# A two-layer transformer block on one core: the stages of the first pass stand in another order on the five engines

## The chip, the cores and the metric

The kernel runs on one core of a Trainium2 chip. The metric is the time of one execution in microseconds (us), as the median of three runs. Lower is better.

The core has engines that each work through a queue of instructions of their own, strictly in the order in which the program put them there: TensorE (PE: matrix products and transposes), VectorE (DVE), ScalarE (ACT: exponentials, other functions and copies), GpSimd (POOL), and SyncE (SP), which here only issues transfers. An engine that comes to a wait stands until a semaphore has the value asked for, and all behind it stands too.

## The reference

Two layers over 2 x 1024 tokens of 256 features. In each layer attention and a feed-forward part both read the normalised input, and both are added to it:

```python
xn = _layernorm(x)
x = x + _L0_attn_ref(xn, Wq, bq, ..., bo) + _L0_ffn_ref(xn, w_gating, w_linear)
xn = _layernorm(x)
x = x + _L1_attn_ref(xn, wq, wk, wv, wo, inv_freq) + _L1_ffn_ref(xn, w_gate_up, w_proj)
...
# _L0_attn_ref: 32 query heads and 8 key/value heads of 8 features, rotary, causal over all 1024 tokens
scores = jnp.einsum('bhqd,bhkd->bhqk', q, k_rep) / scale
scores = jnp.where((kpos > qpos)[None, None], -jnp.inf, scores)
attn = jax.nn.softmax(scores, axis=-1)
# _L0_ffn_ref: fp8 operands
activations = jax.nn.gelu(_qdot(x, w_gating[0])) * _qdot(x, w_gating[1])
outputs = _qdot(activations, w_linear)
# _L1_attn_ref: for each token, 16 heads attend to the 16 heads of the same token
scores = jnp.einsum('bshd,bstd->bsht', q, k) / jnp.sqrt(jnp.float32(HD))
# _L1_ffn_ref: weights quantised to three values per group of 64, silu gate, rms norm
h = jax.nn.silu(gate) * up
return jnp.einsum('bsh,dh->bsd', rms_norm(h), wq_p)
```

## The kernel before

The 2048 tokens are 16 tiles of 128. The work on a tile is cut into stages, each a small function of the kernel, and a step is a stage with a number, as `qk.119` or `wo1.8`. Where a stage comes once per tile the number is the tile's.

Layer 0, attention: `ln0`, `rs0` and `xn` normalise; `xnT` transposes on PE, `xnTc` copies the result out of PSUM (L1178, L1180); `qkv` projects (L625, L626), `qkvc` adds the bias; `rope` (POOL) rotates; `qh`, `ql`, `q0` and `kl` split into parts for 16-bit products; `qxT` turns them and `kTc`, `qTc` copy them out. The scores are computed in 144 quads, two for each pair of a query tile and a key tile at or before it: `qk.Q` (PE, L685, four products of 512 columns, one into each of the four banks of psS), `exp.Q` (ACT, L958, two instructions over two banks each), `mask.Q` on the diagonal (POOL, L1645), and `pv.Q` (PE, L699, eight records in the trace). `qk.Q+1` may write its first two banks only when the first half of `exp.Q` has read them, and its last two when the second half has. So ACT is never more than one quad behind PE, and never ahead. `ob`, `obT`, `att`, `attT`, `wo0` and `xa` finish the attention of a tile.

Layer 0, feed-forward: `up` (L736) four times a tile, `g`, `sq`, `ge1`, `th`, `fh`, `ge3` for the gelu, `down` (L750), `yff`, `xf`. The weights come as six pieces: SP's `wg.k` loads one into half of the tile `stage` (L495, L498), DVE's `w8.k` makes it fp8 (L1104). `up` waits for four of them.

Layer 1: `ln1`, `rs1`, `xn1`, `xn1T`, `xn1Tc`; `qkv1` (L775); `qk1c`, `v1c`, `ro1`, `ro1p`, `ro2`; a way through DRAM (`vw`, `vr`); `gT` (L788), `S1` (L821), `ex1` (L1016), `PV1` (L832), `o1r`, `o1T`, `o1`, again through DRAM (`ow`, `at1r`), `at1T`, `wo1` (L853, L854). Its feed-forward: `gu` (L866), `tg`, `sg`, `hh`, `ssq`, `ssm`, `rsg`, `hxa`, `hx`, `hxT` (L876), `hTc`, `dn1` (L885), and then `yo`, `yout`, `out`. Once: `tc`, `ts`, `tsc`, `td`, `tde`, `tr`, `tw` quantise the weights of that part; `wh` (ACT, L995) and `wl` split the weights of `qkv1`, which a transfer has brought (L484; its semaphore also counts the transfer of wo1, L485); `tab` and `sin` (L924) make the table of angles; `vz` (L1067) clears the tile of values.

What stands where in each engine's queue is written out by hand in the dictionary `ORDER`: one string of steps for each engine, 791 on PE, 421 on ACT, 692 on DVE, 146 on POOL and 88 on SP. Each engine walks its string:

```python
ahead = e.mark_branch_hint_location()
for name, n in first_pass("pe"):
    run[name](n)
```

Each step makes its own waits. Most PE stages fill one of three PSUM banks (psA, psB, psC) in turn, in the order of the string, and wait until the fill three places before has been read:

```python
if k >= len(psM):
    before, number = fills[k - len(psM)]
    w.wait_ge(*EMPTIED[before](number))
```

A second pass with other stages runs only if a flag asks for it; in these runs it doesn't.

Matmuls are of three shapes: over the whole array (most stages), in four groups of 32 rows (`qk`, `S1`), and in four groups of 32 columns (`pv`, `PV1`). The prediction calls a change from one shape to another a shape change.

Of the kernel before, what the change touches and what calls it, by code (L numbers as in the profile page):

```python
# [49 lines left out]
        "xnT.0 qkv.0 ts.0 xnT.1 xnT.2 qkv.1 ts.1 qxT.0 qxT.1 qk.0 xnT.3 qk.1 qkv.2 up.0 up.1 up.2 qxT.2 pv.0 qxT.3 "  # L50
        "up.3 qk.2 pv.1 qk.3 pv.2 qk.4 pv.3 qk.5 obT.0 pv.4 qkv.3 qxT.4 qxT.5 qk.6 pv.5 td.0 xnT.4 qk.7 pv.6 up.4 "
        "td.1 up.5 qk.8 tr.0 pv.7 attT.0 qk.9 pv.8 obT.1 qk.10 pv.9 up.6 up.7 qk.11 down.0 tr.1 xnT.5 attT.1 qkv.4 "
        "qxT.6 ts.2 up.8 qxT.7 up.9 pv.10 pv.11 qk.12 ts.3 up.10 qkv.5 qk.13 pv.12 wo0.0 qk.14 pv.13 down.1 qk.15 "
        "qxT.8 xnT.6 up.11 pv.14 qk.16 pv.15 wo0.1 qk.17 pv.16 up.12 td.2 pv.17 qk.18 td.3 qkv.6 qk.19 tr.2 qxT.9 "
        "up.13 down.2 tr.3 up.14 obT.2 pv.18 pv.19 qk.20 ts.4 ts.5 xn1T.0 obT.3 qk.21 pv.20 up.15 qk.22 qxT.10 pv.21 "
        "up.16 up.17 qk.23 td.4 td.5 up.18 up.19 tr.4 tr.5 attT.2 pv.22 qk.24 xn1T.1 qxT.11 pv.23 ts.6 ts.7 qkv1.0 "
        "wo0.2 qk.25 pv.24 td.6 td.7 up.20 tr.6 qk.26 tr.7 attT.3 down.3 pv.25 qk.27 ts.8 ts.9 gu.0 pv.26 qk.28 "
        "pv.27 up.21 td.8 td.9 qk.29 xnT.7 tr.8 tr.9 pv.28 qk.30 qxT.12 wsum.0 wsum.1 qkv1.1 ts.10 ts.11 pv.29 qk.31 "
        "up.22 pv.30 qk.32 up.23 obT.4 pv.31 qk.33 pv.32 td.10 td.11 wo0.3 tr.10 tr.11 gu.1 gu.2 attT.4 qk.34 pv.33 "
        "gu.3 qk.35 gu.4 qkv.7 qk.36 pv.34 pv.35 gT.0 down.4 gT.1 gu.5 qk.37 gu.6 pv.36 qk.38 qkv1.2 hxT.0 xnT.8 "  # L60
        "S1.0 pv.37 qxT.13 xn1T.2 hxT.1 qk.39 gu.7 qkv1.3 xnT.9 up.24 qk.40 pv.38 pv.39 PV1.0 qk.41 qxT.14 gu.8 "
        "qkv.8 o1T.0 pv.40 qk.42 up.25 xnT.10 qkv1.4 wo0.4 gu.9 xn1T.3 qk.43 pv.41 gT.2 gu.10 up.26 pv.42 qk.44 gT.3 "
        "qkv1.5 at1T.0 qkv1.6 up.27 qk.45 pv.43 pv.44 qxT.15 up.28 gu.11 qk.46 gu.12 up.29 wo1.0 S1.1 pv.45 pv.46 "
        "qk.47 up.30 dn1.0 qk.48 pv.47 hxT.2 down.5 qk.49 gT.4 up.31 xn1T.4 pv.48 qk.50 gT.5 hxT.3 pv.49 qk.51 pv.50 "
        "PV1.1 S1.2 qxT.16 qkv.9 o1T.1 qk.52 pv.51 qkv1.7 up.32 qk.53 up.33 obT.5 pv.52 qk.54 PV1.2 pv.53 qk.55 "
        "attT.5 o1T.2 down.6 gu.13 at1T.1 qk.56 pv.54 pv.55 wo1.1 obT.6 gu.14 gu.15 qk.57 pv.56 up.34 qxT.17 qk.58 "
        "xnT.11 dn1.1 gT.6 up.35 qk.59 pv.57 pv.58 up.36 hxT.4 hxT.5 qk.60 up.37 qkv.10 qkv1.8 gT.7 down.7 qk.61 "
        "pv.59 pv.60 xnT.12 up.38 up.39 qk.62 at1T.2 qkv1.9 wo0.5 gu.16 S1.3 qxT.18 wo1.2 pv.61 qk.63 pv.62 gu.17 "
        "qk.64 pv.63 up.40 up.41 qk.65 pv.64 qxT.19 up.42 qk.66 pv.65 gu.18 gT.8 qk.67 dn1.2 qk.68 pv.66 pv.67 gT.9 "
        "up.43 hxT.6 qk.69 pv.68 PV1.3 qk.70 attT.6 up.44 down.8 hxT.7 S1.4 pv.69 pv.70 qk.71 xn1T.5 wo0.6 o1T.3 "  # L70
        "up.45 qk.72 qkv1.10 gu.19 qk.73 pv.71 qkv.11 down.9 qk.74 pv.72 PV1.4 pv.73 qk.75 at1T.3 xnT.13 up.46 gu.20 "
        "up.47 qk.76 pv.74 pv.75 qxT.20 wo1.3 obT.7 qxT.21 o1T.4 qk.77 dn1.3 attT.7 gu.21 pv.76 qk.78 gu.22 up.48 "
        "pv.77 qk.79 up.49 obT.8 gu.23 hxT.8 qkv.12 xn1T.6 pv.78 qk.80 at1T.4 qkv1.11 up.50 gu.24 attT.8 qk.81 pv.79 "
        "pv.80 wo0.7 hxT.9 obT.9 qk.82 up.51 down.10 qkv1.12 pv.81 qk.83 qxT.22 qxT.23 qkv.13 qk.84 pv.82 down.11 "
        "up.52 xn1T.7 pv.83 qk.85 wo1.4 pv.84 qk.86 attT.9 wo0.8 xnT.14 qxT.24 pv.85 pv.86 qk.87 dn1.4 up.53 qk.88 "
        "gu.25 gu.26 obT.10 pv.87 qk.89 qkv1.13 qkv1.14 qxT.25 up.54 qk.90 pv.88 up.55 hxT.10 gu.27 pv.89 qk.91 "
        "hxT.11 gu.28 gT.10 qk.92 pv.90 wo0.9 attT.10 pv.91 qk.93 gT.11 gT.12 qkv1.15 xn1T.8 qkv.14 up.56 xnT.15 "
        "S1.5 pv.92 pv.93 qk.94 qxT.26 qxT.27 gT.13 gu.29 gu.30 obT.11 qk.95 pv.94 PV1.5 qk.96 up.57 qkv1.16 S1.6 "
        "attT.11 gu.31 up.58 wo0.10 qk.97 pv.95 xn1T.9 up.59 qkv1.17 o1T.5 qk.98 pv.96 pv.97 gT.14 gT.15 qk.99 pv.98 "
        "PV1.6 gu.32 S1.7 o1T.6 down.12 at1T.5 qk.100 pv.99 qxT.28 wo1.5 hxT.12 dn1.5 hxT.13 qk.101 qxT.29 gT.16 "  # L80
        "qkv1.18 at1T.6 qk.102 pv.100 PV1.7 pv.101 qk.103 qkv1.19 up.60 o1T.7 gT.17 wo1.6 dn1.6 S1.8 pv.102 pv.103 "
        "qk.104 gu.33 hxT.14 hxT.15 qk.105 pv.104 down.13 qk.106 obT.12 up.61 pv.105 qk.107 gu.34 gu.35 qk.108 "
        "pv.106 pv.107 gu.36 at1T.7 qk.109 pv.108 qkv.15 qk.110 pv.109 wo1.7 attT.12 qk.111 pv.110 xn1T.10 up.62 "
        "up.63 qk.112 pv.111 PV1.8 qk.113 hxT.16 wo0.11 dn1.7 qk.114 pv.112 pv.113 gT.18 gu.37 gT.19 o1T.8 gu.38 "
        "qk.115 gu.39 pv.114 qk.116 pv.115 qkv1.20 qk.117 hxT.17 wo0.12 gu.40 S1.9 pv.116 pv.117 qk.118 qkv1.21 "
# [1697 lines left out]
```

## Time and profile before

| what | us |
|---|---|
| three runs | 598.49, 600.28, 602.88 |
| median | 600.28 |
| span of the profiled execution | 601.7 |
| PE busy | 562.0 |
| ACT busy | 469.6 |
| DVE busy | 426.6 |
| POOL busy | 233.6 |

The profiled execution is a single one. Its record gives its span, from the first instruction to the last, and no other time for it; the span is 1.4 us above the median and inside the range of the three runs, so what lies around it is too small to be told from the scatter. Busy times overlap between engines. Ends of matmuls are modelled: the record of a matmul lasts longer than the distance to the next start, so a stall shorter than about that overhang hides inside busy time. For PE the distances from start to start tell more than the busy share.

### The profile page before, as it was taken

The page shows a single profiled execution, that of the slowest core. Times are in us where ns is not written, and L with a number is a line of the kernel's source. Part 1 is how long each engine was busy: PE and PEld are TensorE (multiplying, and loading weights), DVE is VectorE, ACT ScalarE, POOL GpSimd, SP SyncE. Part 2 cuts the span into 40 slices and gives each one's busy share as a digit, 9 for nine tenths or more (in the row PEclk, how much of TensorE's full clock was granted, in tenths as well). Part 3 has the DMA queues.
Part 4 walks back from the last instruction along what each step waited for, and adds up shares of the span by engine and source line. Part 5 has one row for each costly group of instructions (what it writes and reads, how often), then busy time and mean ns, then how long its engine had stood idle before and what let it go on. Part 6 is the DMA issues. An engine that isn't in the chain of part 4 may idle for free. (4 is left out here: it accounts for less than half of the span.)

```text
span 601.7 us, 13300 instructions
## 1 busy us (share of the span) xinstructions
PE 562.0 (93%) x5153; PEld 290.7 (48%) x5153; DVE 426.6 (71%) x909; ACT 469.6 (78%) x607; POOL 233.6 (39%) x302
## 2 busy tenths in 40 slices
PE   3687898999999999999999999999999999999976
PEld 1332434433555555645544555565445454456654
DVE  5658889988789558856699877565555365658765
ACT  2378899999988997999878898777979877972631
POOL 3748666043533163306855641360232150250100
PEclk9778999999999999999999999999999999999989
DMA  8810101102041223030110330531301304035632
GB/s 265 303 36 2 36 1 35 36 2 49 6 62 33 33 59 39 27 37 3 19 17 2 64 54 27 89 55 27 54 10 36 45 20 69 17 68 85 94 57 48
DMA packets 150914, 30.40 MB, mean 51 GB/s; under 512 B 133952, under 2 KB 149568, under 8 KB 150848
## 3 DMA queue, kind: packets, MB, share of 16 engines
q1 hardware_dynamic: 150272, 29.19, 24.4%
q8 instruction: 42, 0.69, 0.5%
q10 hardware_dynamic: 576, 0.33, 0.3%
q14 instruction: 24, 0.20, 0.1%
HBM read 19.02 MB, written 10.49 MB: 49 GB/s over the span
## 5 line engine op out<-in xcount | busy, mean ns | idle before, releaser
L958 ACT ACTIVATE Pt<-psS 128x1024 f32<-128x1024 f32 x288 | 281.7, 1047 | 44.8 <-PE psS L685 25.9
L699 PE MATMUL psV<-Pt,vaug 128*32 128x512 f32 x1152 | 150.3, 611 | 0.3 <-POOL Pt L1645 0.3
L1645 POOL TENSOR_SCALAR_AFFINE_SELECT Pt<-Pt 128x1024 f32<-128x1024 f32 x64 | 71.7, 1145 | 43.8 <-ACT Pt L958 43.8
L685 PE MATMUL psS<-qTf,kTf 32*128 32x512 f16 x576 | 74.9, 390 | 7.3 <-ACT Pt L958 3.7
L685 PEld LDWEIGHTS psS<-qTf,kTf 32*128 32x128 f16 x576 | 20.3, 91 | 82.9 <-ACT Pt L958 48.1
L1695 POOL TENSOR_TENSOR ss<-ss,mhalf 128x1 f32<-128x1 f32 x16 | 9.5, 596 | 111.3 <-DVE ss L1476 111.3
L699 PEld LDWEIGHTS psV<-Pt,vaug 128*32 128x32 f32 x1152 | 25.7, 109 | 41.9 <-issue 35.9
L1016 ACT ACTIVATE stage<-psS 128x1024 f32<-128x1024 f32 x32 | 31.0, 1020 | 8.1 <-PE psS L821 7.9
L1686 POOL TENSOR_TENSOR r<-qk,cos 128x256 f32<-128x256 f32 x16 | 11.9, 744 | 63.9 <-ACT qk L991 58.0
L866 PE MATMUL psB<-wguT,xhs 128*128 128x512 bf16 x108 | 27.8, 380 | 0.0
L1032 ACT ACTIVATE qtmp<-qtmp 128x1024 bf16<-128x1024 f32 x16 | 16.9, 1059 | 12.9 <-PE psA L876 8.4
L1318 DVE SCALAR_TENSOR_TENSOR gw<-gw,gb 128x512 f32<-128x512 f32 x32 | 24.9, 781 | 2.5 <-ACT gw L973 2.5
L1327 DVE SCALAR_TENSOR_TENSOR ga<-gw,gb 128x512 bf16<-128x512 f32 x32 | 23.6, 738 | 3.9 <-ACT gw L984 3.8
L1636 POOL TENSOR_TENSOR QXf<-rt,QXf 128x512 f16<-128x512 f32 x16 | 19.1, 1195 | 18.1 <-ACT QXf L945 18.1
L1608 POOL TENSOR_SCALAR rs<-mv 128x1 f32<-128x1 f32 x16 | 5.3, 329 | 49.6 <-DVE mv L1164 49.6
L1625 POOL TENSOR_TENSOR rt<-qkv,cs 128x320 f32<-128x320 f32 x16 | 14.7, 916 | 24.5 <-DVE QXf L1220 15.8
L984 ACT ACTIVATE gw<-gw 128x512 f32<-128x512 f32 x32 | 21.2, 661 | 3.0 <-DVE gw L1318 2.9
L1482 DVE SCALAR_TENSOR_TENSOR qtmp<-qtmp,ss 128x1024 f16<-128x1024 f32 x16 | 21.4, 1336 | 2.9 <-ACT qtmp L1037 2.9
L866 PE MATMUL psC<-wguT,xhs 128*128 128x512 bf16 x88 | 22.8, 382 | 0.0
L973 ACT ACTIVATE gw<-gb 128x512 f32<-128x512 bf16 x32 | 21.2, 670 | 0.1
L885 PE MATMUL psA<-wpT,stmp 128*128 128x256 bf16 x176 | 21.1, 273 | 0.0
L1628 POOL TENSOR_TENSOR rt<-qkv,sn 128x160 f32<-128x160 f32 x32 | 20.9, 673 | 0.0
(381 smaller groups left out, 1246.5 us busy)
## 6 DMA issues: line engine op xcount, KB each, us to landing
qkvscr<-rqkv SPq DMA_DIRECT2D x16, 384.0 KB, 2.5
G<-qkvscr SPq DMA_DIRECT2D x24, 128.0 KB, 3.7
stage<-in_wg SPq DMA_DIRECT2D x4, 512.0 KB, 8.8
w8g<-qkvscr SPq DMA_DIRECT2D x16, 128.0 KB, 3.8
oscr<-o SPq DMA_DIRECT2D x16, 128.0 KB, 3.3
at<-oscr SPq DMA_DIRECT2D x16, 128.0 KB, 2.0
out<-yout SPq DMA_DIRECT2D x16, 128.0 KB, 2.5
x<-in_x SPq DMA_DIRECT2D x1, 1536.0 KB, 12.2
```

Of the source, the lines that this page charges most:

```text
L685: e.matmul(psS[j], kd[32 * j:32 * j + k, h, 128 * at:128 * at + 128], qd[32 * j:32 * j + k, 4 * h:4 * h + 4, :].rearrange("p s n -> p (s n ...
L699: ins = e.matmul(psV[32 * j:32 * j + 32, :], vaug[:, at, j, 32 * h:32 * h + 32], Pt[(4 * Q + j) % NP], start=(kb == 0 and h == 0), stop=(k ...
L866: ins = e.matmul(bank[:], src[:, pt, 128 * c:128 * c + 128], wguT[:, c, c0:c0 + 512], start=(k == 0), stop=(k == 3))
L885: ins = e.matmul(bank[:, 0:256], hT[:, pt, s, :], wpT[:, s, :], start=(k == 0), stop=(k == 15))
L958: e.activation(flat(Pt4[:, u % NP:u % NP + 2, :]), flat(psS4[:, j:j + 2, :]), ACT.Exp, scale=scale).then_inc(S["exp"], 1)
L973: e.activation(gw[:, half, :], gb[:, half, :], ACT.Square).then_inc(S["sq"], 1)
L984: e.activation(gw[:, half, :], gw[:, half, :], ACT.Tanh, scale=GC * GA).then_inc(S["th"], 1)
L1016: e.activation(P1[:, 4 * b:4 * b + 8, :].rearrange("p g n -> p (g n)"), flat(psS4[:, b:b + 2, :]), ACT.Exp, scale=SC1).then_inc(S["ex1"], 1)
L1318: e.scalar_tensor_tensor(gw[:, half, :], gw[:, half, :], 1.0 / GA, gb[:, half, :], ALU.add, ALU.mult).then_inc(S["ge1"], 1)
L1327: e.scalar_tensor_tensor(a, gw[:, half, :], 1.0, gg, ALU.add, ALU.mult).then_inc(S["ge3"], 1)
L1482: e.scalar_tensor_tensor(hx_b[:, 1, :], h1, sn[:, 2:3], hx_b[:, 0, :], ALU.mult, ALU.subtract).then_inc(S["hx"], 1)
L1645: e.affine_select(out=p, in_=p, pattern=[[0, 8], [1, 128]], compare_op=ALU.is_ge, fill=0.0, base=0, channel_multiplier=-1).then_inc(S["mas ...
```

## The change

Only the strings of `ORDER` differ. Each holds the same steps, and steps of one stage keep their own sequence; 34 to 87 steps of each string stand at the same place as before, the others have moved, on PE by 3.9 places on average and by 32 at most. The bank that a PE stage fills follows from its place, so many stages use another of the three banks than before. The file is four lines shorter, so that line L958 of before is L954 in the changed kernel, and so on for all lines behind the strings.

```diff
 ORDER = {
     "pe": (
-        "xnT.0 qkv.0 ts.0 xnT.1 xnT.2 qkv.1 ts.1 qxT.0 qxT.1 qk.0 xnT.3 qk.1 qkv.2 up.0 up.1 up.2 qxT.2 pv.0 qxT.3 "
...
+        "xnT.0 qkv.0 xnT.1 qkv.1 xnT.2 qxT.0 qxT.1 qk.0 ts.0 ts.1 up.0 qk.1 qxT.2 qkv.2 qxT.3 pv.0 qk.2 up.1 xnT.3 "
...
     "sp": (
-        "wt.2 wg.2 wg.3 wg.4 wg.5 wt.3 wt.4 wt.5 vw.0 vr.0 vw.1 vr.1 ow.0 at1r.0 vw.2 vr.2 vw.3 ow.1 at1r.1 out.0 "
...
+        "wg.2 wg.3 wg.4 wg.5 wt.2 wt.3 wt.4 wt.5 vw.0 vr.0 vw.1 ow.0 at1r.0 vr.1 vw.2 vr.2 ow.1 at1r.1 vw.3 vr.3 out.0 "
...
```

ACT at the start, before: the two instructions of `tc.0`, then `qh.0`, the four of `exp.0` and `exp.1`, `qh.1`, `g.0`, `fh.0`.

```order
L931 ACTIVATE qtmp<-r 128x1024
L932 ACTIVATE qtmp<-r 128x1024
L945 ACTIVATE QXf<-rt 128x32x16
L958 ACTIVATE Pt<-psS 128x1024 x4
L945 ACTIVATE QXf<-rt 128x32x16
L966 ACTIVATE gb<-psC 128x512
```

The same place now; the row over 1536 columns is `wh.0`.

```order
L927 ACTIVATE qtmp<-r 128x1024
L928 ACTIVATE qtmp<-r 128x1024
L941 ACTIVATE QXf<-rt 128x32x16
L991 ACTIVATE wqkv<-stmp 128x1536
L954 ACTIVATE Pt<-psS 128x1024 x2
L941 ACTIVATE QXf<-rt 128x32x16
L962 ACTIVATE gb<-psA 128x512
```

`wh.0` has moved from the 61st place of ACT's string to the third, ahead of `exp.0`. `sin.0`, which was the 17th step, is the 102nd.

DVE between the bias of the first tile and the copies of the second, before (`qkvc.0`, `xnTc.1`, `xn.3`, `tsc.0`, `w8.0`, `xnTc.2`, `w8.1`):

```order
L1189 TENSOR_TENSOR qkv<-psB,bqkv 128x384
L1178 COPY xnT<-psA 128x256
L1180 CAST x8T<-psA 128x256
L1171 TENSOR_SCALAR xn<-x,mv_1,rs_1 128x256
L1130 TENSOR_SCALAR qtmp<-psC 128x512
L1104 CAST w8g<-stage 128x1024
L1178 COPY xnT<-psB 128x256
L1180 CAST x8T<-psB 128x256
L1104 CAST w8g<-stage 128x1024
```

And now:

```order
L1185 TENSOR_TENSOR qkv<-psB,bqkv 128x384
L1100 CAST w8g<-stage 128x1024 x2
L1174 COPY xnT<-psC 128x256
L1176 CAST x8T<-psC 128x256
L1167 TENSOR_SCALAR xn<-x,mv_0,rs_0 128x256
```

Both casts `w8.0` and `w8.1` now stand ahead of `xnTc.1`; `vz.0`, which stood between `ln0.0` and `xn.0`, is now the first step of DVE.

PE in the last quarter, from `qk.119` to `qk.120`, before: `PV1.9` and `pv.118` stand between them.

```order
L685 MATMUL psS<-qTf,kTf 128x512 x4
L832 MATMUL psC<-stage,w8l 32x128 x16
L699 MATMUL psV<-Pt,vaug 32x512 x4
L685 MATMUL psS<-qTf,kTf 128x512 x4
L699 MATMUL psV<-Pt,vaug 32x512 x4
```

And now, with `wo1.8`, `xn1T.11` and `pv.118` between them:

```order
L681 MATMUL psS<-qTf,kTf 128x512 x4
L849 MATMUL psC<-wo,at1T 128x256
L850 MATMUL psC<-wo,at1T 128x256
L586 MATMUL psA<-identf,xn_1 128x128
L587 MATMUL psA<-identf,xn_1 128x128
L695 MATMUL psV<-Pt,vaug 32x512 x4
L681 MATMUL psS<-qTf,kTf 128x512 x4
```

`PV1.9`, of the same shape as `pv.118`, has gone from beside it, and two stages over the whole array have come.

## Rows read from the trace of the kernel before

**Rows 1.** The page: span, and busy time of each engine.

```profile
span 601.7 us, 13300 instructions
PE 562.0 (93%) x5153; PEld 290.7 (48%) x5153; DVE 426.6 (71%) x909; ACT 469.6 (78%) x607; POOL 233.6 (39%) x302
```

**Rows 2.** Busy time by stretch: stretch, length, PE, PEld, DVE, ACT, POOL, clock, DMA, GB/s.

```profile
0.00:22.20 22.20, 8.93 (x27) 4.31 (x28) 14.05 (x35) 3.92 (x4) 10.24 (x25) 1.00 0.94 304
22.20:48.10 25.90, 21.02 (x130) 8.70 (x130) 14.44 (x36) 18.43 (x24) 15.09 (x16) 0.74 0.25 90
48.10:111.35 63.25, 56.85 (x464) 24.80 (x465) 56.93 (x108) 59.01 (x82) 40.74 (x51) 0.97 0.06 18
111.35:225.95 114.60, 113.06 (x1032) 54.97 (x1029) 86.44 (x187) 105.56 (x139) 43.17 (x56) 1.00 0.21 37
225.95:532.70 306.75, 303.05 (x2851) 156.60 (x2850) 204.59 (x433) 255.22 (x325) 113.01 (x142) 1.00 0.23 37
532.70:602.00 69.30, 59.07 (x659) 41.29 (x657) 50.19 (x113) 27.44 (x37) 11.32 (x16) 0.98 0.39 66
```

**Rows 3.** Timeline of PE: start, length, instruction, count of records.

```profile
405.66 0.61 PE L736 MATMUL psC<-x8T,w8g 128*128 128x128 fp8e4 x8
406.11 0.61 PE L841 MATMUL psA<-identf,o1r 128*128 128x128 f32 x4
...
407.93 1.91 PE L885 MATMUL psA<-wpT,stmp 128*128 128x256 bf16 x16
409.77 1.17 PE L821 MATMUL psS<-qk1T 24*128 24x128 f32 x32
...
591.50 1.91 PE L885 MATMUL psA<-wpT,stmp 128*128 128x256 bf16 x16
593.25 0.27 PE L590 MATMUL psB<-identf,at 128*128 128x128 f32 x1
```

**Rows 4.** Timeline from qk.119 to qk.120, with idle time before and its releaser.

```profile
460.18 0.53 PE L685 MATMUL psS<-qTf,kTf 32*128 32x512 f16 x4
460.64 1.94 ACT L958 ACTIVATE Pt<-psS 128x1024 f32<-128x1024 f32 x2 [0.37 <-PE psS L685]
...
461.54 1.04 PE L699 MATMUL psV<-Pt,vaug 128*32 128x512 f32 x8
462.51 0.21 PEld L685 LDWEIGHTS psS<-qTf,kTf 32*128 32x128 f16 x4 [0.84 <-ACT Pt L958]
```

**Rows 5.** Timeline of the start, all engines.

```profile
1.25 0.41 SPq L470 DMA_DIRECT2D wqkv<-in_wqkv  x1
...
4.87 2.19 DVE L1067 MEMSET vaug<- 128x2560 f32 x1 [0.48 <-issue]
...
7.86 0.45 SPq L495 DMA_DIRECT2D stage<-in_wg  x1
...
10.63 1.62 PE L625 MATMUL psB<-wqkv,xnT 128*128 128x384 f32 x2 [2.23 <-DVE xnT L1178]
...
14.63 0.59 SPq L485 DMA_DIRECT2D wo<-in_wo  x1
...
22.64 3.77 ACT L958 ACTIVATE Pt<-psS 128x1024 f32<-128x1024 f32 x4 [4.17 <-PE psS L685]
...
25.98 0.69 DVE L1104 CAST w8g<-stage 128x1024 fp8e4<-128x1024 f32 x1 [3.93 <-DMA stage<-in_wg]
...
35.55 1.02 ACT L958 ACTIVATE Pt<-psS 128x1024 f32<-128x1024 f32 x1 [0.16 <-PE psS L685]
```

**Rows 6.** Transfers issued at 1.25, 7.86 and 14.63 us: size, us to landing.

```profile
wqkv<-in_wqkv SPq DMA_DIRECT2D x1, 384.0 KB, 6.5
...
stage<-in_wg SPq DMA_DIRECT2D x1, 512.0 KB, 7.5
...
wo<-in_wo SPq DMA_DIRECT2D x1, 256.0 KB, 8.8
```

**Rows 7.** ACT by line: busy, mean ns, idle before.

```profile
L995 ACT ACTIVATE wqkv<-stmp 128x1536 f16<-128x1536 f32 x1 | 1.7, 1677 | 0.0
L924 ACT ACT_TABLE_LOAD x1 | 1.3, 1283 | 0.0
```

255 rows, old and new, of the table ORDER are left out of this document.

## The prediction, made before the run

> **What bounds the kernel now.** I read the page first. PE is busy 562.0 of 601.7 us, ACT 469.6, DVE 426.6 [rows 1]. Then the busy time by stretch, cut where `qk.0`, `qk.6`, `qk.24`, `qk.56` and the end of the quads stand: the reader is to see that PE is busy 113.06 of 114.60 us and 303.05 of 306.75 us in the two middle stretches, but 8.93 of 22.20, 21.02 of 25.90 and 59.07 of 69.30 at the ends [rows 2]. PE bounds the middle, and the waits of start and end are chains through several engines.
>
> Busy isn't packed, though. In the timeline `qk.120` starts 2.33 us after `qk.119`, where its weight load has waited for ACT's exponentials of the quad before, and the busy share doesn't show it [rows 4]. A quad's two exponentials take 1.94 us [rows 4], and since the four score banks hold one quad only, `qk.Q+1` can't finish its writes sooner. So two things make PE's time in the middle: the work itself, and stalls at `qk` where ACT is late.
>
> **Prices on PE**, from start to start. Eight matmuls of 128 columns take 0.45 us, 405.66 to 406.11 [rows 3]. Sixteen of 256 columns take 1.75, 591.50 to 593.25, when a stage of the same shape follows, and 1.84, 407.93 to 409.77, when one of four row groups does [rows 3]: a shape change costs 0.09. `pv` with the change to `qk` behind it is 0.97, 461.54 to 462.51 [rows 4]; I take 0.87 and 0.1. Four row groups run together, so a `qk` is one stream of 512 columns; from the 128-column price that is 4 x 0.056, or 0.22 (an estimate). In this way each stage gets its number of columns times 0.44 ns. On ACT a quad is 1.94, `wh` 1.7 [rows 7], the other stages 0.6 to 1.2 by their width. All PE stages are priced at the full clock.
>
> With these I added up the written-out strings, once for each order. In each gap from one `qk` to the next, P is the PE work with its shape changes, A the ACT work from one `exp` to the next. Where A is over P, ACT falls behind; E is the sum of what it is over.
>
> - qk.6 to qk.24: P 50.2 before, 49.4 now; E 20.9, now 14.2. It took 63.25 [rows 2], so 13.0 were stalls.
> - qk.24 to qk.56: P 105.2, now 110.6; E 17.8, now 18.7. It took 114.60 [rows 2], stalls 9.4.
> - qk.56 to the last quad: P 283.8, now 282.9; E 31.8, now 19.4. It took 306.75 [rows 2], stalls 23.0.
>
> **The start, up to qk.6.** No row shows the new order, so I walk it with the prices of the old. `vz` (2.19 us [rows 5]) leaves the way of the first normalisation and runs while DVE would wait for its first data. The first projection could then start when its weights have landed, at 1.25 + 6.5 = 7.75, and not at 10.63 [rows 5, 6]: a gain of 2.9. The gain is held up twice. `w8.1` now stands ahead of `xnTc.1`, and its piece lands at 7.86 + 7.5 = 15.4 [rows 5, 6]; with the cast (0.69 [rows 5]) DVE goes on at about 16.1, so the second tile is no earlier than before and `qk.0` comes at about 22.5. And `wh.0` stands ahead of `exp.0`. It waits for both transfers of its semaphore, the last at 14.63 + 8.8 = 23.4 [rows 5, 6], and takes 1.7: `exp.0` starts at 25.1, where it was 22.64 [rows 5]. That costs 2.5.
>
> After that the new order is the looser one. Before, `exp.2` came only at 35.55 [rows 5], since DVE stood 3.93 us for the third piece of weights [rows 5], `up.0` to `up.2` stood ahead of `pv.0` on PE, and three of ACT's stages of the first `up`s stood behind that. Now one `up` stands there. In my walk kl.1 is done at 28.6, ql.1 on POOL at 29.5 (it has slipped behind both masks of `mask.0`), and `exp.2` starts near 32; `qk.6` comes near 45, with `wh` and one `th` out of the way, where it was at 48.1 [rows 2]. The walk is an estimate and can be 3 us off. Its bounds: a loss of the 2.5 if all behind `exp.0` keeps its distance, a gain of the 4.9 us in which PE is idle in this stretch, 25.90 less 21.02 [rows 2]. I take -3.
>
> The two table loads around `sin.0` (1.3 each [rows 7]) and its two instructions, 3.2 in all, stood ahead of `exp.6` and stand ahead of `exp.32` now, so they are in A of 24 to 56. They are neither saved nor added. Their cover there is ACT's idle time, 114.60 less 105.56 [rows 2]. Without it they would show fully.
>
> **The middle.** The bounds for each stretch: above, stalls go in proportion to E; below, only those go that the order forces, where P is under 2.3 us, the time from `qk` to `qk` that the exponentials need [rows 4]. There are 41 such gaps from qk.6 on, short by 6.1 us together, now 16, short by 2.6.
>
> - 6 to 24: in proportion 49.4 + 13.0 x 14.2 / 20.9 = 58.2, that is -5.0; the lower bound is -0.8 of work and -0.7 of short gaps, -1.5. I take -3.2.
> - 24 to 56: in proportion 110.6 + 9.9 = 120.5, +5.9; with the short gaps alone +5.4 - 0.9 = +4.5. I take +5.2.
> - 56 on: in proportion 282.9 + 14.0 = 296.9, -9.9; with the short gaps alone -0.9 - 1.9 = -2.8. I take -6.4.
>
> The middle of the bounds is a choice: some stalls have nothing to do with ACT, and E doesn't see them.
>
> P holds the shape changes. I counted them along PE's string: 431 before, 468 now, so 37 x 0.1 = 3.7 us more, which the sums above contain. A stage like PV1.9 has been taken from beside a `pv` of its own shape, as in the piece shown. The Trainium skill (TensorEngine Tiling (Array Packing), Tiling Modes) says it outright: "Changing tiling mode (not just tile) drains the TensorE". It names no price. By that rule alone, all else equal, the change would lose the 3.7.
>
> **The end.** The chain behind the last quad has the same work within 0.3 us (53.5 and 53.2 in my sum) in 69.3 us [rows 2]. `S1` and `ex1` of tiles 13 to 15 stand a little earlier, which helps the way through DRAM; `PV1.11` and `qkv1.28` are now behind the last quad, which doesn't. I take 0, with 2 us either way. The flag steps, now last, run while the last output is on its way.
>
> **Sum.** -3 (start) - 3.2 + 5.2 - 6.4 (middle) + 0 (end) = -7.4. The profiled span of 601.7 becomes 594.3. The median of the runs lies 1.4 under that span, so I say 593.
>
> **Rivals.**
>
> *Only PE's work counts* (chance 0.18). If ACT's lateness is absorbed, and stalls stay as they are, the middle changes by P alone, -0.8 + 5.4 - 0.9 = +3.7, and the start gives -3: about 601 on the median's scale, within 598 to 604. For it speaks PE's 99% in the middle [rows 2]; against it the waiting load at `qk.120` [rows 4].
>
> *Stalls follow E fully* (0.15). The upper bounds together: -3 - 5.0 + 5.9 - 9.9 = -12.0, with a start and an end 2 better each perhaps; 585 to 589.
>
> *`wh.0` holds up the whole start* (0.13), the case on the other side. All exponentials queue behind one transfer. If it lands at 23.4 or later and `exp.2` then keeps its distance to `exp.0` (which it does if mask.0 and ql.1 on POOL are the chain, from `exp.2` later than 35.55 on), the start loses 2.5 instead of gaining 3; with +3.7 of work that is not won back, 601.7 + 2.5 + 3.7 - 1.4 = 606.5.
>
> *The shape changes alone* (0.06). If neither start nor stalls move, 37 changes at the price of [rows 3] are left: 3.7 us more, 604, within 1%. This is what the Trainium skill's rule on tiling modes (same page and section) makes of the time when it is taken alone; the 0.09 that this trace shows agrees with the rule.
>
> **How the numbers follow.** My forecast is 589 to 598, with 593 as its centre and a chance of 0.48. A difference under 1% (6 us) can hardly be told from none with these runs. Under 594.3 lie the bigger gain, 0.15, and most of the lower half and centre of the forecast, 0.35: faster 0.50. Over 606.3 lies half of the wh case and little else; since the whole could drift in a way that no sum shows, I give slower 0.12, and the same 0.38. The range goes from 585, the full effect of E, to 604, where only work and drains count.
>
> **What the profile after would show.** `exp.0` at about 25, waiting through `wh.0` for a transfer; `qk.0` near 22.5; DVE standing about 3 us ahead of `w8.1`. `qk.6` near 45; qk.6 to qk.24 in about 60, qk.24 to qk.56 in about 120, the rest to `qk.143` in about 300. PE's waits for ACT ahead of `qk` are shorter in total. I am wrong if `exp.2` isn't ahead of 35.55, if the last long stretch takes 306 again, or if DVE or POOL, for which I added up nothing in the middle, now holds PE.

## The result, and the profile after

The changed kernel takes 631.41 us (median of 4 runs, 628.3 to 633.8) against 599.57 us: a ratio of 1.051, with an interval of 1.046 to 1.056. It is slower, and the forecast of 593 (585 to 604) was wrong by more than its range.

The page of the changed kernel, its first lines (beside [rows 1]), and the costliest groups of section 5. The changed kernel's line numbers are four lower than the old one's:

```profile
span 632.0 us, 13299 instructions
PE 562.5 (89%) x5153; PEld 288.8 (46%) x5153; DVE 452.0 (72%) x909; ACT 472.3 (75%) x607; POOL 241.9 (38%) x302
...
L954 ACT ACTIVATE Pt<-psS 128x1024 f32<-128x1024 f32 x288 | 279.5, 1026 | 57.1 <-PE psS L681 50.6
L695 PE MATMUL psV<-Pt,vaug 128*32 128x512 f32 x1152 | 154.7, 619 | 3.4 <-DVE ob L1286 3.3
L1641 POOL TENSOR_SCALAR_AFFINE_SELECT Pt<-Pt 128x1024 f32<-128x1024 f32 x64 | 76.2, 1215 | 92.0 <-ACT Pt L954 92.0
```

The same 909 instructions of DVE are busy 25.4 us longer. Nothing was added to them, so they last longer on the average: an engine was slowed, not loaded. POOL's masks last longer too; this is their line in the old kernel:

```profile
L1645 POOL TENSOR_SCALAR_AFFINE_SELECT Pt<-Pt 128x1024 f32<-128x1024 f32 x64 | 71.7, 1145 | 43.8 <-ACT Pt L958 43.8
```

Busy time by stretch, cut as in [rows 2] (start to `qk.0`, `qk.6`, `qk.24`, `qk.56`, `qk.143`, end), but each cut 0.25 us behind the quad's own start; columns as there:

```profile
0.00:21.58 21.58, 8.86 (x28) 4.52 (x28) 13.26 (x35) 3.92 (x4) 9.73 (x24) 0.84 0.91 310
21.58:50.35 28.77, 18.82 (x142) 8.22 (x138) 22.93 (x36) 19.03 (x25) 23.95 (x25) 0.78 0.23 83
50.35:113.41 63.06, 56.05 (x448) 24.32 (x444) 55.75 (x114) 54.32 (x74) 37.08 (x44) 0.94 0.06 18
113.41:245.10 131.69, 121.13 (x1066) 58.06 (x1064) 100.05 (x194) 112.48 (x146) 47.48 (x58) 0.96 0.20 34
245.10:560.48 315.38, 299.05 (x2828) 152.72 (x2824) 207.64 (x421) 256.31 (x325) 113.31 (x140) 0.98 0.21 35
560.48:632.00 71.52, 58.63 (x659) 40.94 (x655) 52.32 (x114) 26.26 (x35) 10.36 (x15) 0.97 0.38 64
```

From the quads' own starts (21.33, 50.10, 113.16, 244.85 and 560.23) the way to `qk.6` is 2.0 us longer than in the old kernel (-0.9 to `qk.0` and +2.9 behind it), the quads 6 to 24 take 0.2 less, the quads 24 to 56 17.1 more, 56 to 143 8.6 more, and the end 2.8 more. In the fourth stretch PE is idle for 10.6 us, where it was idle for 1.5. The granted clock is 0.96 and 0.98 in the fourth and fifth stretch, where it was 1.00.

One place shows how. The timeline of the changed kernel from 187.66 us, four engines (start, length, instruction; in brackets the idle time before it and who ended it):

```profile
188.13 2.32 POOL L1641 TENSOR_SCALAR_AFFINE_SELECT Pt<-Pt 128x1024 f32<-128x1024 f32 x2
...
188.26 1.24 DVE L1409 TENSOR_TENSOR rqkv<-r 128x256 f32<-128x256 f32 x1
...
189.42 1.30 DVE L1411 TENSOR_TENSOR rqkv<-r 128x256 f32<-128x256 f32 x1
...
190.83 0.43 DVE L1402 TENSOR_TENSOR r<-qk,sin 128x256 f32<-128x256 f32 x1
190.87 0.98 POOL L1682 TENSOR_TENSOR r<-qk,cos 128x256 f32<-128x256 f32 x1 [0.42 <-DVE rqkv L1411]
191.17 0.96 DVE L1403 TENSOR_TENSOR r<-qk,cos 128x256 f32<-128x256 f32 x1
...
192.05 0.55 DVE L1185 TENSOR_TENSOR qkv<-psC,bqkv 128x384 f32<-128x384 f32 x1
...
192.65 0.50 PEld L716 LDWEIGHTS psC<-wo,attT 128*128 128x128 f32 x2 [3.72 <-DVE qkv L1185]
192.65 1.22 PE L716 MATMUL psC<-wo,attT 128*128 128x256 f32 x2 [3.48 <-DVE qkv L1185]
193.66 1.06 PE L717 MATMUL psC<-wo,attT 128*128 128x256 f32 x2
194.52 1.06 PE L732 MATMUL psA<-x8T,w8g 128*128 128x128 fp8e4 x8
195.37 1.06 PE L732 MATMUL psB<-x8T,w8g 128*128 128x128 fp8e4 x8
196.36 1.92 PE L695 MATMUL psV<-Pt,vaug 128*32 128x512 f32 x8
198.22 0.40 PE L681 MATMUL psS<-qTf,kTf 32*128 32x512 f16 x4
```

In the old kernel the second of the two instructions of `ro2` stands at this length, and so does the first:

```profile
170.10 0.42 DVE L1415 TENSOR_TENSOR rqkv<-r 128x256 f32<-128x256 f32 x1
```

Read it from above. POOL's two masks run to 190.45, one behind the other, and the two instructions of `ro2`, 0.42 us in themselves, take 1.24 and 1.30. The second one of `ro1` takes 0.96 instead of 0.43: POOL's L1682 ends at 191.85, DVE's at 192.13, 0.28 later. `qkvc.8` stands behind all of them in DVE's row, bank psC isn't read until then, and `wo0.4` on PE waits 3.48 us for it. Of these the stretch of the three makes 2.2 (0.82 + 0.88 + 0.53 over their usual lengths); the rest is what else stands ahead of `qkvc.8`. Then PE works at the lower of its two clock levels for 5.6 us: eight fp8 products take 1.06 us, where they took 0.61 [rows 3], and a `pv` takes 1.92 instead of 1.04 [rows 4]. By the prices of the forecast this quad took about 6.5 us over its work, for one wait of 3.5.

**The 0.28 us come back everywhere.** I took for each line of DVE the length that its quickest fifth has, and listed each instruction over 0.12 us longer. There are 95 (53.1 us above their usual length), and 94 of them have an instruction of POOL beside them. 81 end a constant time after one of POOL's, to within 0.02 us, and the time is set by their own length: 0.28 us for the 43 of 0.42 or 0.43, 0.55 for the 20 of 0.68, 0.15 for the 7 of 0.28. Such a DVE instruction does its work only once POOL's has ended. The old kernel has 59 of them, with 27.9 us; under the masks alone it is 8.8 us before and 22.7 now.

Not every DVE instruction is held up so. In the changed kernel 235 of them start while one of POOL's has 0.2 us or more left. Of these, 111 read a PSUM bank and 20 are batch statistics, reductions and reciprocals in SBUF: none of the 131 is stretched. Of the other 104, which work from SBUF to SBUF, 86 are. `qkvc.8` in the rows above is of the first kind and keeps its usual 0.55 us beside POOL; it is late only by what stands ahead of it. So the steps that empty a bank aren't slowed themselves here: they are late behind others that are.

And it works in both directions. A mask takes 1.09 us at its usual length; 21 of the 64 take over 0.12 us more (7.5 us together; in the old kernel 7, with 3.2 us), and each of the 21 ends 0.95 us after the end of a DVE instruction. In this place the two engines hold each other up in turn:

```profile
139.68 2.58 POOL L1641 TENSOR_SCALAR_AFFINE_SELECT Pt<-Pt 128x1024 f32<-128x1024 f32 x2
...
139.90 1.41 DVE L1323 SCALAR_TENSOR_TENSOR ga<-gw,gb 128x512 bf16<-128x512 f32 x1
...
141.41 1.12 DVE L1326 TENSOR_TENSOR ga<-ga,fb 128x512 bf16<-128x512 bf16 x1
```

The first mask ends at 140.77, L1323 0.54 later at 141.31, the second mask 0.95 later at 142.26, and L1326 0.27 later at 142.53.

The Trainium skill (SBUF — State Buffer, Who interferes with whom) has this rule: the two engines share one pair of ports as an exclusive lock, held for the whole instruction, against a DVE instruction in a two-port mode or with two inputs in SBUF. Its "fully blocks (not throttle)" agrees with the constant 0.28 us.

The other waits are in the list of PE's waits over the changed kernel (us in total, times, the longest); in the old one no single wait behind the first normalisation and projection is longer than 1.8 us:

```profile
PE psC L716 <- DVE qkv L1185: 3.5, 1, 3.5
PE psV L695 <- DVE ob L1286: 3.3, 4, 1.6
PE psS L681 <- ACT Pt L954: 3.1, 4, 1.3
PE psA L784 <- DMA G<-qkvscr: 2.9, 1, 2.9
...
PE psB L784 <- DMA G<-qkvscr: 2.5, 1, 2.5
PE psC L586 <- DMA at<-oscr: 2.4, 1, 2.4
```

### The profile page after: what moved, and what is told of

It is laid out like the page before. It is cut to its first block, busy times and chain, and to the rows that moved or that the text cites. A ratio compares the mean times of both kernels' runs of the same rounds, so it can differ in the third digit from the quotient of the medians.

```text
span 632.0 us, 13299 instructions
## 1 busy us (share of the span) xinstructions
PE 562.5 (89%) x5153; PEld 288.8 (46%) x5153; DVE 452.0 (72%) x909; ACT 472.3 (75%) x607; POOL 241.9 (38%) x302
## 4 chain that ended last, share of the span: by engine, by line
PE 60%; DVE 19%; DMA 9%; issue 5%; SPq 3%; ACT 3%; DVEq 0%; ACTq 0%
PE psV L695 15%; PE psS L681 5%; DMA stage<-in_wg 3%; PE psC L862 2%; PE psB L862 2%; DMA G<-qkvscr 2%; DMA w8l<-qkvscr 2%; DVE ga L1326 2%; PE psA L862 2%; PE psS L817 2%; DVE ga L1323 2%; SPq L518 2%; DMA qkvscr<-rqkv 2%; PE psC L881 1%; PE psB L771 1%
## 5 line engine op out<-in xcount | busy, mean ns | idle before, releaser
L954 ACT ACTIVATE Pt<-psS 128x1024 f32<-128x1024 f32 x288 | 279.5, 1026 | 57.1 <-PE psS L681 50.6
L695 PE MATMUL psV<-Pt,vaug 128*32 128x512 f32 x1152 | 154.7, 619 | 3.4 <-DVE ob L1286 3.3
L1641 POOL TENSOR_SCALAR_AFFINE_SELECT Pt<-Pt 128x1024 f32<-128x1024 f32 x64 | 76.2, 1215 | 92.0 <-ACT Pt L954 92.0
L681 PE MATMUL psS<-qTf,kTf 32*128 32x512 f16 x576 | 61.2, 392 | 4.6 <-ACT Pt L954 3.1
L681 PEld LDWEIGHTS psS<-qTf,kTf 32*128 32x128 f16 x576 | 16.1, 91 | 75.8 <-ACT Pt L954 43.7
L1682 POOL TENSOR_TENSOR r<-qk,cos 128x256 f32<-128x256 f32 x16 | 12.6, 789 | 68.9 <-ACT qk L987 61.8
L1323 DVE SCALAR_TENSOR_TENSOR ga<-gw,gb 128x512 bf16<-128x512 f32 x32 | 26.1, 817 | 6.3 <-ACT gw L980 6.2
L1314 DVE SCALAR_TENSOR_TENSOR gw<-gw,gb 128x512 f32<-128x512 f32 x32 | 26.8, 838 | 1.8 <-ACT gw L969 1.8
L862 PE MATMUL psB<-wguT,xhs 128*128 128x512 bf16 x92 | 24.4, 389 | 0.0
L1326 DVE TENSOR_TENSOR ga<-ga,fb 128x512 bf16<-128x512 bf16 x32 | 21.8, 680 | 3.3
L1330 DVE CAST a<-ga 128x512 fp8e4<-128x512 bf16 x32 | 21.7, 679 | 1.1
## 6 DMA issues: line engine op xcount, KB each, us to landing
x<-in_x SPq DMA_DIRECT2D x1, 1536.0 KB, 12.1
```

The source lines that it names most:

```text
L681: e.matmul(psS[j], kd[32 * j:32 * j + k, h, 128 * at:128 * at + 128], qd[32 * j:32 * j + k, 4 * h:4 * h + 4, :].rearrange("p s n -> p (s n ...
L695: ins = e.matmul(psV[32 * j:32 * j + 32, :], vaug[:, at, j, 32 * h:32 * h + 32], Pt[(4 * Q + j) % NP], start=(kb == 0 and h == 0), stop=(k ...
L862: ins = e.matmul(bank[:], src[:, pt, 128 * c:128 * c + 128], wguT[:, c, c0:c0 + 512], start=(k == 0), stop=(k == 3))
L954: e.activation(flat(Pt4[:, u % NP:u % NP + 2, :]), flat(psS4[:, j:j + 2, :]), ACT.Exp, scale=scale).then_inc(S["exp"], 1)
L1314: e.scalar_tensor_tensor(gw[:, half, :], gw[:, half, :], 1.0 / GA, gb[:, half, :], ALU.add, ALU.mult).then_inc(S["ge1"], 1)
L1323: e.scalar_tensor_tensor(a, gw[:, half, :], 1.0, gg, ALU.add, ALU.mult).then_inc(S["ge3"], 1)
```

## The experiments

All kernels were compared with the old one on the same chip; it took 599.7 to 601.2 us beside them. The changed kernel ran only in the first comparison, so where an experiment is set against its 631.4 us, a difference of 2 us isn't clear of noise. The kernels of an experiment have the old kernel's line numbers, or up to a few more. "Small mask" kernels leave seven eighths of the causal mask out.

### Where the loss is made: four splices

```diff
# a24b, a60b: each engine's string = its changed order up to the last step that had started
#             when qk.24 (qk.60) began in the trace, then the rest in the old order
# b24a, b56a: the old order up to qk.24 (qk.56), then the rest in the changed order
```

> The changed order on every engine up to the steps that had started when quad 24's scores began (its first 24 quads of 144), the old order for all that is left. Theory P (the loss is made where the trace shows it: +2.1 us up to quad 24, +17.1 from 24 to 56, +8.6 from 56 to 143, +2.2 after): this kernel keeps only the first +2.1 us, so 602 us (600 to 604). Rival H (the start leaves behind something that the rest pays for, such as buffers and queues in another phase, DRAM transfers behind): 610 us or more.

> The old order up to quad 24's scores, the changed order for the rest. Theory P: the whole of the middle's and the end's loss, 600 + 17.1 + 8.6 + 2.2 = 628 us (625 to 631). Rival H: under 615 us.

> The changed order up to quad 60's scores, the old order for the rest. At quad 60 the changed kernel was 16.7 us behind. Theory P: 600 + 16.7 = 617 us (614 to 620). Rival H: 622 us or more, or the old order makes some of it good (under 612 us) where its waits had slack.

> The old order up to quad 56's scores, the changed order for the rest. Theory P: 600 + 8.6 + 2.2 = 611 us (608 to 614). Rival H (the tail stretch's own loss came from the 19 us of lateness that it took over): 600 to 604 us.

Measured: a24b 608.9 us (1.012 to 1.019 of the old kernel), b24a 629.7 (1.043 to 1.051), a60b 621.2 (1.032 to 1.037), b56a 622.7 (1.035 to 1.039). Compared with the old kernel at the same quads in the traces (the end is that of PE's last matmul), in us:

```
              quad 24   32     48     56     80     110    130    143    end
changed         1.8    8.6   18.1   18.9   19.2   19.8   29.5   27.5   31.1
b24a           -2.1    7.1   12.6   13.5   13.8   15.7   23.8   21.9   26.9
a60b            1.9    9.8   16.6   17.5   16.1   16.1   16.1   16.1   14.1
b56a           -0.6   -0.6   -0.6   10.5   10.3   10.9   18.4   16.4   18.6
a24b            6.2    7.1    6.9    6.9    6.7    6.7    6.7    6.7    4.6
```

The old order behind a seam holds its distance to a tenth of a us over 60 quads (a60b, 80 to 143), and the changed order makes its losses at the same places, whatever ran before. So theory P holds by the traces, with b24a inside its range in time. By the times alone it isn't as clear: a60b is 1 us above P's range and 1 under the rival's 622, and the other two expectations missed, a24b by 7 (it is nearer to the rival's 610) and b56a by 12 us. Both lose it in the quads just ahead of the seam (7.9 us from quad 12 to 24, and 11.1 from 48 to 56), where two orders that don't fit each other meet. A splice has a price of its own, and only the stretches away from its seam can be read.

### The masks, and the named waits

```diff
# after_small_mask, before_small_mask
-e.affine_select(out=p, in_=p, pattern=[[0, 8], [1, 128]], ...
+e.affine_select(out=p[:, 0:1, :], in_=p[:, 0:1, :], pattern=[[0, 1], [1, 128]], ...
# after_later_gathers: TensorE's string
-... hxT.12 gT.16 qxT.28 pv.100 qk.102 hxT.13 qxT.29 ...
+... hxT.12 qxT.28 pv.100 qk.102 hxT.13 qxT.29 gT.16 ...
# (gT.20 behind wo0.13, gT.22 behind pv.132 likewise; on VectorE gTq.10 two steps later)
# after_banks_first: VectorE's string, the first two of eight moves
-... ro2.1 ro1.2 qkvc.8 ...        -... ge3.21 sg.10 ...
+... qkvc.8 ro2.1 ro1.2 ...        +... sg.10 ge3.21 ...
```

> The changed kernel with the causal mask put on the first 128 of each 1024 columns only (the other seven eighths stay unmasked, so this part of the computation is left out): GpSimd's 128 mask instructions of the first pass shrink from about 1.2 us to some 0.3 us, everything else stays. Theory C (GpSimd's instructions, when they run beside VectorE's, stretch them: line 1326's 0.42 us to 0.9 us; in the changed order the masks fall on VectorE's long steps, and the emptying of TensorE's banks behind them comes late): the changed kernel gains far more from it than the old one does, 618 us or less here. Rival O (the order of the rows alone makes banks and transfers late, the stretch is a bystander): 626 to 632 us.

> The old kernel with the same cut (the mask on the first 128 of 1024 columns, the rest left out). Theory C: little to gain, 597 to 601 us, so that the distance to the changed kernel with the same cut falls from 31 us to 20 us or less. Rival O: the distance stays at 27 to 32 us.

> The changed kernel with three of its transposes of gathered tiles later in TensorE's row: gT.16 and gT.22 one to two quads later, gT.20 one quad later (and VectorE's gTq.10 two steps later with it). These three waited 2.5, 2.9 and 1.2 us for the gathering DMA, and the first two were followed by 3.6 and 5.8 us at the lower clock. Theory L (each loss is local, and the lower clock is its echo): 6.6 us of waits and some 4.7 us of the lower clock go, 620 us (618 to 624). Rival N (whoever is late next takes the time): 627 us or more.

> The changed kernel with eight steps of VectorE that empty TensorE's banks taken out from behind long steps and put ahead of them: qkvc.8 before ro2.1, wmin.0 before tw.6, sg.10 before ge3.21, hTc.8 before ge3.22, sg.11 before xn.14, yff.11 before ge3.25, xa.9 before ge3.26, hh.21 before xn1.12. TensorE's waits for them were 3.5, 1.7, 0.8, 1.0, 1.8, 1.2, 1.3 and 0.8 us, 12.1 us together, and 5.6 us at the lower clock followed the first. Theory L: 617 us (614 to 621). Rival N: 627 us or more.

Measured: 608.7 and 598.0 us for the small masks, 627.4 for the later gathers, 629.4 for the banks first. With small masks the changed order gains 22.7 us and the old one 3, and the distance falls from 31 to 10.7 us: theory C. The page of the changed order with small masks has DVE back at the busy time of the old kernel with whole masks, though not one of its instructions was touched:

```profile
span 609.6 us, 13299 instructions
PE 558.4 (92%) x5153; PEld 288.3 (47%) x5153; DVE 425.9 (70%) x909; ACT 471.7 (77%) x607; POOL 189.3 (31%) x302
```

The moves at the named waits gave 4 and 2 us where theory L had promised 11 and 14; with single runs from 625.1 to 631.6 the 2 us can't be told from nothing. In after_banks_first `wo0.4` waits no more, and behind it a product of `up` waits 2.75 us for the next DVE step of the same row. For 12.1 us of waits for DVE the time fell by 2. Rival N has it: a row that is late hands its lateness to the next step.

### Is it the stretch, or GpSimd's own row?

```diff
# after_small_mask_idle_work: behind each small mask
+for i in range(2):
+    w.wait_ge("dummy", len(dummies))
+    dummies.append(Q)
+    e.affine_select(out=idle[:, 0:448], in_=idle[:, 0:448], pattern=[[1, 448]], ...).then_inc(S["dummy"], 1)
# before_more_idle_work: the same behind each whole mask of the old kernel
# after_small_mask_one_long: instead of the two
+e.tensor_tensor(idle[:], idle[:], idle[:], ALU.add).then_inc(S["dummy"], 1)
# after_mask_halves, before_mask_halves (n = 4), after_mask_quarters (n = 2): whole masks in pieces
-e.affine_select(out=p, in_=p, pattern=[[0, 8], [1, 128]], ...
+for h in range(0, 8, n):
+    ins = e.affine_select(out=p[:, h:h + n, :], in_=p[:, h:h + n, :], pattern=[[0, n], [1, 128]], ...
```

> The changed kernel with the mask on the first 128 of 1024 columns only (the rest unmasked, so left out), and after each of these short masks GpSimd does two masks of 448 columns on a tile that nobody reads. TensorE gets its tile as early as with the small mask alone (608.7 us), but GpSimd is busy about as long as with the whole mask (631 us). Theory C (GpSimd's busy time beside VectorE is what costs): 622 us or more, and VectorE's line 1330 back from 0.43 us towards 0.68 us. Rival W (TensorE waited for the masks' results): 608 to 613 us.

> The old kernel with its masks whole, and behind each the same two masks of 448 columns on a tile that nobody reads: GpSimd works about 60 us more in the first pass. Theory C: the old order isn't proof against it but has more slack, since its masks stretched VectorE by only 8.6 us against 22.7 in the changed order; 604 to 615 us. Rival P (the old order puts nothing of VectorE near the masks by its nature): 600 to 603 us.

> The changed kernel, each whole mask of 1024 columns issued as two instructions of 512 (nothing left out). Theory E (a VectorE instruction that meets one of GpSimd's does its work only after that one has ended, so the length of one instruction counts): the masks' 22.7 us of stretch fall to about 12 and the time from 631 us to 618 to 625 us. Rival R (GpSimd's row is what is late): the row gets some 0.15 us longer per mask, 631 to 636 us.

> The old kernel with each mask issued as two instructions of 512 columns. Theory E: 598 to 601 us (with small masks it gained 3 us). Rival R: 601 to 605 us.

> The changed kernel with each mask issued as four instructions of 256 columns; GpSimd's mask time grows by about a third. Theory E: the stretch under masks falls to some 7 us; 612 to 622 us. Rival R: 634 us or more.

> As after_small_mask_idle_work (mask on 128 of 1024 columns, the rest left out), but the idle work behind each small mask is one addition of 512 bfloat16 columns (about 1.2 us) instead of two masks of 448 (0.6 us each); GpSimd is as busy. Theory E: VectorE's stretch goes from 31 us to 40 us or more and the time from 616.7 to 621 us or more. Rival R: 614 to 618 us, as with the two short ones.

Measured, with the stretch worked out as above (all of it, and what lies under the masks or under the idle work in their place) and the busy times of the page:

```
                              time    DVE busy  stretch  under them  POOL busy
changed kernel                631.4    452.0     53.1      22.7       241.9
after_mask_halves             624.6    441.7     43.3      15.6       254.6
after_mask_quarters           625.6    430.7     29.4       7.5       273.4
after_small_mask_one_long     621.4    440.4     41.5      17.4       261.4
after_small_mask_idle_work    616.7    430.9     31.3       8.7       265.3
after_small_mask              608.7    425.9     26.8     under 1     189.3
old kernel                    600      426.6     27.9       8.8       233.6
before_mask_halves            600.3    424.0     25.0       5.1       243.6
before_more_idle_work         649.0    437.2     37.8      19.5       311.0
before_small_mask             598.0    418.5     18.8     under 1     182.3
```

The halves were 7 us faster with 13 us more of POOL's time, as theory E has it and rival R excludes (1.034 to 1.044 of the old kernel, against 1.046 to 1.056). The quarters fulfil E's forecast for the stretch (7.5, forecast 7) and miss that for the time, 625.6 (one of four runs 631.6) instead of 612 to 622. Their list of PE's waits says what came in its place, POOL itself, which the changed kernel had at 0.2:

```profile
PE psV L699 <- POOL Pt L1646: 14.9, 14, 2.5
```

So both causes are real: the stretch of DVE, and a row of POOL that is itself late. With the idle work as one long instruction, an addition, the stretch is 10 us larger and the median 4.7 us later than with two short ones, although POOL is busy 4 us less; their single runs overlap (614.8 to 622.1 against 613.1 to 621.0), and they ran beside different measurements of the old kernel (601.1 and 599.7), so this pair only leans to E. After_small_mask_idle_work itself fell between its two forecasts, at 616.7. The idle work costs 8 us over small masks alone, with only 4.5 us more of stretch in all; the other 15 of the 22.7 went with the stretch and with the masks' earlier results, which these runs don't part.

Before_more_idle_work missed by far: I had expected 604 to 615. It took 649.0, and not by the stretch (10 us more), but because the idle work stands ahead of the next mask:

```profile
PE psV L700 <- POOL Pt L1648: 25.1, 15, 3.3
```

The old order isn't proof against a slow GpSimd. It is fitted to this one.

### The rest

```diff
# after_small_mask_gathers_sin: small mask, the three later gathers, and ScalarE's string
-... exp.20 ... exp.31 sin.0 g.11 exp.32 ...
+... exp.20 ... sin.0 exp.21 ... exp.31 g.11 exp.32 ...
# after_gathers_banks_sin: whole masks, with the eight moves of after_banks_first as well
# after_small_mask_gathers_old_tail: small mask, gathers, sin.0 not moved; from qk.143 on the old order
```

> The changed kernel with the small mask (seven eighths of it left out), the three later transposes of gathered tiles (gT.16, gT.20, gT.22, with gTq.10), and the step with the two sines ahead of quad 21's exponential instead of quad 32's. With the small mask alone 608.7 us; TensorE's waits for the gathers were 3.1, 2.8 and 1.5 us there with the lower clock behind two of them, and 1.3 us for the exponential behind the sines. If these are the rest of the distance to the old kernel with the small mask (598.0 us): 598 to 601 us. If others take their place: 605 us or more.

> The changed kernel, whole masks, with all the moves so far: the three later transposes, the eight bank emptyings ahead of long steps, and the sines earlier. Alone the first gave 4 us and the second 2 us. Theory C: while the masks stretch VectorE, moving its steps only passes the wait on, 621 to 626 us. Rival O (order alone): the moves act together once none is left to take over the wait, 612 us or less.

> The changed kernel with the small mask (seven eighths left out) and the three later transposes of gathered tiles, and from quad 143's scores on the old order on every engine. Theory T (the end's own order makes the loss there): the last stretch takes 64 to 65 us again instead of 71.0, the time 599 to 602 us. Rival D (the stretch before leaves a debt of transfers and GELU steps): the last stretch takes 68 us or more, 604 to 608 us.

Measured: 607.1, 625.4 and 600.3 us. The second is what moves of the order alone can do while the masks stretch DVE: 6 us of 31. The first gave only 1.6 us for the gathers and the sines, and its profile shows why. From quad 56 to 143 it took 303.5 us, where small masks alone gave 308.9 and the old kernel with small masks 305.5; but from `qk.143` to PE's last matmul it took 71.0 against 63.6. Its timeline has the end's own gathers there:

```profile
561.58 1.08 PE L788 MATMUL psC<-identf,G 128*128 128x128 f32 x4 [1.83 <-DMA G<-qkvscr]
574.72 0.33 PE L590 MATMUL psC<-identf,at 128*128 128x128 f32 x1 [2.49 <-DMA at<-oscr]
```

With the old order behind `qk.143` that stretch is 62.9 us and the time 600.3 (0.995 to 1.003 of the old kernel): theory T. With that the distance to before_small_mask (598.0) is down to 2.3 us. (Theory T had 64 to 65 us for the stretch.) No kernel here that computes the reference beats the old one; the best, before_mask_halves, is the same within its interval (0.997 to 1.002).

## Why the prediction was wrong

**The term that was missing.** The forecast said that it "added up nothing in the middle" for DVE and POOL, and named that as the way it would fail. That is the step that failed. I priced PE and ACT in each gap, and left DVE out because it had slack on the average (86.44 of 114.60 us [rows 2]). But the emptying of a bank isn't an average: it stands in one row, behind steps whose length depends on what POOL does at that moment. About 20 of the 31 us go with the masks: with small ones a distance of 10.7 is left. How much of the 20 is DVE's stretch and how much POOL's own lateness is open; the halves show that at least part of it, 7 us, is the stretch. The lower clock behind a long stall makes it dearer: between quads 24 and 143 the changed kernel works in four spells of 3.2, 5.6, 3.6 and 5.8 us at the lower level, behind PE's waits of 1.3 (the sines), 3.5, 2.5 and 2.9 us, and does half the work there. The old kernel has no such spell between these quads.

**The start, -3.** The first part of the walk was right: `qk.0` at 21.33 (forecast 22.5), `exp.0` near 24.2 (25.1) behind `wh.0`, which waited for its transfer, and `exp.2` ahead of its old 35.55, at 32.92 (32). Rows of ACT in the changed kernel, to be read against [rows 5]:

```profile
22.76 1.48 ACT L991 ACTIVATE wqkv<-stmp 128x1536 f16<-128x1536 f32 x1 [7.68 <-DMA wo<-in_wo]
24.15 1.92 ACT L954 ACTIVATE Pt<-psS 128x1024 f32<-128x1024 f32 x2
...
32.92 1.94 ACT L954 ACTIVATE Pt<-psS 128x1024 f32<-128x1024 f32 x2 [2.30 <-PE psS L681]
```

So the rival in which `wh.0` holds up the whole start is out: `exp.0` came 1.5 us later than before (priced at 2.5), and `exp.2` 2.6 earlier. But `qk.6` came at 50.1, not 45, behind a copy that took 1.08 us for 0.18 beside a mask and GELU steps of 1.37 and 1.20 for 0.68. With small masks it came at 45.6, near the forecast, but there the old kernel has 46.6; and four more profiled executions with small masks and the same order up to there have 45.2, 46.2 and, with idle work, 47.1 and 48.6. So of the -3 no gain is shown that is clear of this scatter, and with whole masks it is a loss of 2.0. A walk that prices each DVE step at its usual length finds the place and not the order's worth.

**Quads 6 to 24, -3.2.** Measured -0.2; with small masks 60.6 against 62.1, -1.5, the lower bound (60.6 is one execution; two others have 58.4 and 61.1).

**Quads 24 to 56, +5.2.** Measured +17.1, and +8.6 with small masks. If the work term of +5.4 is right, the rest of the 8.6 are stalls that the sum by ACT's excess doesn't see, as `wmin.0` (1.7 us at `ts.8`).

**The sines, neutral.** Not quite. ACT's two table loads (1.28 each) and sines stood between two exponentials, and PE waited 1.3 us for the second (its longest wait for ACT in the list above); the first of the four spells at the lower clock came behind it. Averaged idle time of ACT was named as their cover; it wasn't idle there. Moving them was never measured alone.

**Quads 56 on, -6.4.** Measured +8.6. With small masks alone it is +3.5. With the three gathers later as well it is -2.0 in one execution (303.5 us) and +0.4 in another (305.9, after_small_mask_gathers_old_tail, whose order is the same up to `qk.143`). So even the direction isn't shown. The ACT excess E fell by 12.4 us in the sum, and the stalls went from 21.7 to 20.6 or 23.0. That stalls follow E, on which the -6.4 rests, is not shown by any run, and the rival in which they follow it fully is out. What E could not see cost more: the gathers whose transfers were issued late, as `gT.16` and `gT.20`, 2.5 and 2.9 us of waiting.

**The shape changes, +3.7.** The price holds in the old trace: L885's sixteen products take 1.84 to 1.85 us in six places where four row groups follow, and 1.75 to 1.76 in eight where the whole array does. What 37 more of them cost the kernel no run isolates. PE's busy time in the two profiles is 562.5 and 562.0, with the lower clock in it, and doesn't settle it.

**The end, 0.** Measured +2.8 to the end of the span and +3.6 to PE's last matmul, and by the latter +4.7 and +7.4 in after_small_mask and after_small_mask_gathers_sin. "Stands a little earlier, which helps the way through DRAM" was wrong: the transposes in that stretch wait for their transfers, 1.83 and 2.49 us in the rows above, where the old kernel's longest wait for a transfer behind `qk.143` is 1.7. The old order there gives the time back.

## What to carry to other kernels

Before a reordering, list for every step that empties a buffer what stands ahead of it in its engine's row, and which of those meet an instruction of GpSimd; averages of busy time hide both. A VectorE instruction from SBUF to SBUF that starts beside GpSimd's costs what is left of that one, so short GpSimd instructions do less harm than long ones, until GpSimd's own row becomes the late one. Those that read PSUM passed unharmed here. And when one wait is removed in a row that is late as a whole, expect the next step to wait in its place: take away what makes the row late, not the wait.

## What the runs showed of the hardware

VectorE's delay beside GpSimd isn't proportional to the overlap: the instruction ends 0.28 us (0.42-us instructions) or 0.55 us (0.68-us ones) after GpSimd's, whenever it was started. It holds to 0.02 us for 81 of the 95 stretched instructions, and for 92 of 105 with the masks in halves; nine `xn` steps of 0.40 us end 0.15 us after, as regularly. None of the 111 instructions that read PSUM beside GpSimd was stretched. GpSimd waits in the same way: all 21 stretched masks of the changed kernel end 0.95 us after a VectorE instruction. Undisturbed, a mask of 1024 columns took 1.09 us, of 512 columns 0.63, of 256 columns 0.41 and of 128 columns 0.29 (on the average, beside VectorE, 1.15 to 1.22, 0.67 to 0.73, 0.47 and 0.34 to 0.40). So cutting one mask into four costs GpSimd a half more, 111.2 us for 76.2. And the same order up to quad 20, with small masks, stood between 4.1 and 7.7 us ahead of the old kernel at quad 24 in five profiled executions, two of them with idle work: a single execution's start says nothing about 2 or 3 us.
